# Attention on one core: row maximum of q.k alone in four row groups, the weighted sum in two pieces per head

## The reference

```python
qkv = (x @ w_qkv).reshape(B, L, 3, H, Dh)            # B=4, L=1024, H=16, Dh=8
attn = jnp.einsum('bhid,bhjd->bhij', q, k) * Dh ** (-0.5)
attn = attn + phi_bias(L)[None, None]                # log(exp(-|p_i - p_j|) + 1e-8)
attn = jax.nn.softmax(attn, axis=-1)
out = jnp.einsum('bhij,bhjd->bhid', attn, v)
out = jnp.transpose(out, (0, 2, 1, 3)).reshape(B, L, D)
return out @ w_proj + b_proj
```

## Time and profile before

| | us |
|---|---|
| median of 3 runs | 1227.99 |
| lowest and highest | 1227.91, 1228.85 |
| span of the profiled execution | 1235.2 |
| attend stage, first to last issue of a store | 224.7 to 272.1 |
| attention, first score matmul to last weighted sum | 273.4 to 1016.9 |
| steps 1 to 61 of it | 302.3 to 992.1 |

### The profile page before, as it was taken

How to read it: one execution, slowest core, us unless ns; L and a number is a source line. 1 busy time by engine, 2 the same in 40 slices (tenths; PEclk the granted TensorE clock), 3 DMA queues, 4 the chain that set the end, 5 groups by cost and what they waited for, 6 DMA issues and landing times. The chain is left out here.

```text
span 1235.2 us, 26880 instructions
## 1 busy us (share of the span) xinstructions
PE 1084.3 (88%) x6562; PEld 529.4 (43%) x6563; DVE 933.5 (76%) x1753; ACT 708.5 (57%) x1574; POOL 419.9 (34%) x628
## 2 busy tenths in 40 slices
PE   5549993759999999999999999999999986729997
PEld 4449993422222222222222222222222216629997
DVE  6447774869888888888888888888888817837885
ACT  1024441444777777777777777777777761104443
POOL 2524343443223332323232333323232322642433
PEclk9999997787999999999999999999999996659999
DMA  9221113240111111111111111111111146432221
GB/s 329 97 55 44 41 43 88 96 148 20 30 34 37 32 31 34 36 31 32 35 35 31 31 36 33 31 33 36 32 31 35 28 103 202 164 109 69 67 67 30
DMA packets 54063, 77.03 MB, mean 62 GB/s; under 512 B 15679, under 2 KB 35269, under 8 KB 53368
## 3 DMA queue, kind: packets, MB, share of 16 engines
q1 hardware_dynamic: 48264, 65.25, 18.0%
q0 software_dynamic: 5056, 10.53, 2.3%
q10 hardware_dynamic: 704, 0.79, 0.3%
HBM read 54.61 MB, written 25.41 MB: 65 GB/s over the span
## 5 line engine op out<-in xcount | busy, mean ns | idle before, releaser
L946 DVE TENSOR_REDUCE nmax<-psS 128x1 f32<-128x1024 f32 x512 | 602.9, 1220 | 109.2 <-PE psS L899 109.1
L960 ACT ACTIVATE prob<-psE 128x512 f32<-128x512 f32 x1024 | 537.1, 606 | 179.2 <-PE psE L891 178.9
L899 PE MATMUL psS<-kop,qop 120*128 120x512 bf16 x1024 | 393.8, 388 | 11.6 <-DVE mpart L930 8.6
L891 PE MATMUL psE<-qop,kop 123*128 123x512 bf16 x1024 | 389.1, 382 | 3.4 <-ACT prob L960 2.6
L1004 POOL TENSOR_TENSOR prob<-prob,const 128x512 f32<-128x512 f32 x128 | 162.4, 1269 | 472.5 <-ACT prob L960 472.5
L915 PE MATMUL psV<-prob,vst 128*9 128x512 f32 x2048 | 267.1, 595 | 1.0 <-issue 0.8
L891 PEld LDWEIGHTS psE<-qop,kop 123*128 123x128 bf16 x1024 | 99.3, 98 | 314.1 <-ACT prob L960 219.0
L899 PEld LDWEIGHTS psS<-kop,qop 120*128 120x128 bf16 x1024 | 99.5, 98 | 117.7 <-DVE nmax L946 17.7
L752 ACT ACTIVATE siga<-psGa,w1sa 128x128 f32<-128x128 f32 x156 | 44.5, 368 | 62.9 <-PE psGa L660 62.9
L752 ACT ACTIVATE sigb<-psGb,w1sb 128x128 f32<-128x128 f32 x156 | 44.5, 368 | 60.7 <-PE psGb L660 60.7
L915 PEld LDWEIGHTS psV<-prob,vst 128*9 128x9 f32 x2048 | 30.8, 88 | 109.9 <-issue 109.9
(11 more groups left out here) (163 smaller groups left out, 1023.2 us busy)
## 6 DMA issues: line engine op xcount, KB each, us to landing
qop<-qk_parts SPq DMA_DIRECT2D x192, 48.0 KB
kop<-qk_parts SPq DMA_DIRECT2D x192, 48.0 KB
qk_parts<-part_attend SPq DMA_DIRECT2D x16, 384.0 KB, 2.8
xsb<-sorted_b SPq DMA_DIRECT2D x39, 128.5 KB
weighted_sums<-osum SPq DMA_DIRECT2D x256, 18.0 KB
w1a<-in_w SPq DMA_DIRECT2D x1, 4128.0 KB
w1b<-in_w SPq DMA_DIRECT2D x1, 4128.0 KB
qop<-mrow SPq DMA_DIRECT2D x256, 1.5 KB
```

The lines of the kernel that those rows point to most:

```text
L891: nc.tensor.matmul(psE[BANK[n]][:], kop[b][0:TROWS, kt * P:(kt + 1) * P], qop[b][0:TROWS, cols], start=True, stop=True).then_inc(s_t, 1)
L899: last = nc.tensor.matmul(psS[kt % 2][:, half, :], qop[b][0:SROWS, kt * P:(kt + 1) * P], kop[b][0:SROWS, cols], start=True, stop=True)
L946: nc.vector.tensor_reduce(nmax[r % 2][:, qt:qt + 1], psS[qt % 2][:], AX.XY, ALU.max, negate=True).then_inc(s_max, 1)
L960: nc.scalar.activation(prob[r % 2][:, lo:lo + HALF], psE[BANK[n]][:], ACT.Exp).then_inc(s_exp, 1)
```

## The change

The scores for the maximum no longer contain the bias, and of q and k only four of the nine products of parts: low.low, high.high, high.middle and middle.high. These are 32 rows, and they stand four times in new operands `qS` and `kS` of 128 partitions: the two halves of an even tile and those of an odd tile use the rows from 0, 32, 64 and 96 on. The row maximum is thus that of q.k alone, and it goes into the exponent in two bf16 parts instead of three (122 rows, two removed GpSimd operations). q and k are stored with their parts in sequences ("lhhml" and "hmlhmh") in five and six transfers per group, and every operand of a head comes with one transfer: four per head instead of six, of 256, 256, 144 and 144 KB. The sums are stored whole, with the unused partitions, in one transfer, and read back in eight per batch instead of four. TensorE's order is now by pairs of tiles: exponents of the even tile, scores of both tiles, exponents of the odd tile, and after every second pair two pieces of the weighted sum. In the diff, counts of semaphores and the shape of `pickhead` and `kbias`, which follow from this, are left out.

```diff
@@ -32,8 +32,10 @@
 COMBO = 9 * DH
 BIAS0, BIASN = COMBO, 6 * KT
 MAX0 = BIAS0 + BIASN
-SROWS = MAX0
-TROWS = MAX0 + 3
+TROWS = MAX0 + 2
+QSEQ, KSEQ = "lhhml", "hmlhmh"
+STORES = len(QSEQ) + len(KSEQ)
+SROWS = 4 * DH
 PBLK = L + P
 
 XBUF = 4
...
@@ -261,13 +263,14 @@
                     sp.dma_start(g.kop[n][BIAS0:TROWS, :], d.kbias).then_inc(g.s_init, 16)
                 for n in range(groups):
                     b, c = half(n)
-                    for z in range(2):
+                    for z, (to, seq) in enumerate(((d.q, QSEQ), (d.k, KSEQ))):
                         sp.wait_ge(s_part, 2 * n + z + 1)
-                        sp.dma_start(d.qk[z, :, b * P:(b + 1) * P, c].rearrange("a p t -> p a t"),
-                                     part[:, n % 2, z, :, :]).then_inc(s_out[n % 2], 16)
+                        for at, a in enumerate(seq):
+                            sp.dma_start(to[b * HEADS:(b + 1) * HEADS, at, :, c],
+                                         part[:, n % 2, z, "hml".index(a), :]).then_inc(s_out[n % 2], 16)
                     if n == 1:
                         for s in range(2):
-                            sp.wait_ge(s_out[s], 32)
+                            sp.wait_ge(s_out[s], 16 * STORES)
                     if n in (2, 4, 6):
                         load_head(sp, d, g, n // 2 - 1, n // 2 - 1)
             if not attend:
...
@@ -763,21 +766,27 @@
 
 def load_sums(sp, d, g, b):
 
-    sums = d.sums.rearrange("(b h) a e t -> b a h e t", h=HEADS)
-    for a in range(2):
-        sp.dma_start(g.den[:, b % 2, a, :], sums[b, a, :, DH, :].rearrange("h (j q) -> h j q", q=P))\
-            .then_inc(g.s_den_in[b], 16)
-        sp.dma_start(g.num[:, b % 2, a, :], sums[b, a, :, 0:DH, :]).then_inc(g.s_num_in[b], 16)
+    sums = d.sums.rearrange("(b h) (j e) t -> b j h e t", h=HEADS, j=4)
+    for j in range(4):
+        a, half = j // 2, j % 2
+        sp.dma_start(g.den[half * 64:half * 64 + 64, b % 2, a, :],
+                     sums[b, j, :, DH, :].rearrange("h (j q) -> h j q", q=P)).then_inc(g.s_den_in[b], 16)
+        sp.dma_start(g.num[:, b % 2, a, half * HALF:(half + 1) * HALF], sums[b, j, :, 0:DH, :])\
+            .then_inc(g.s_num_in[b], 16)
 
 
 def load_head(sp, d, g, head, b):
 
-    rows = bass.ds(head * DH, DH)
-    for a in range(3):
-        at = slice(a * 3 * DH, (a + 1) * 3 * DH)
-        sp.dma_start(g.qop[b][at, :], d.qk[0, a, rows, :].unsqueeze(0).to_broadcast([3, DH, L])
-                     ).then_inc(g.s_op[b], 16)
-        sp.dma_start(g.kop[b][at, :], d.qk[1, :, rows, :]).then_inc(g.s_op[b], 16)
+
+    def rows(src, at, parts, repeat, step):
+        size = len(QSEQ if src is d.q else KSEQ) * DH * L
+        return bass.AP(tensor=src.tensor, offset=head * size + at * DH * L,
+                       ap=[[step * DH * L, repeat], [L, parts * DH], [1, L]])
+
+    sp.dma_start(g.qS[b][:], rows(d.q, 0, 4, 4, 0)).then_inc(g.s_op[b], 16)
+    sp.dma_start(g.kS[b][:], rows(d.k, 2, 4, 4, 0)).then_inc(g.s_op[b], 16)
+    sp.dma_start(g.qop[b][0:COMBO, :], rows(d.q, 2, 3, 3, 0)).then_inc(g.s_op[b], 16)
+    sp.dma_start(g.kop[b][0:COMBO, :], rows(d.k, 0, 3, 3, 1)).then_inc(g.s_op[b], 16)
 
 
 def phase_attention(nc, d, g):
...
@@ -848,10 +857,8 @@
 
                 if live(at, -2):
                     sp.wait_ge(s_ev, i - 1)
-                    for j in range(4):
-                        sp.dma_start(d.sums[bass.ds(i - 2, 1), j // 2, :,
-                                            (j % 2) * HALF:(j % 2 + 1) * HALF].squeeze(),
-                                     osum[r % 2][32 * j:32 * j + VW, :]).then_inc(s_os[r % 2], 16)
+                    sp.dma_start(d.sums[bass.ds(i - 2, 1), :, :].squeeze(),
+                                 osum[r % 2][:]).then_inc(s_os[r % 2], 16)
 
                 if live(at, 1):
                     b = (r + 1) % NBUF
...
@@ -860,16 +867,16 @@
 
                         sp.dma_start(qop[b][MAX0:TROWS, :].rearrange("a (t q) -> a t q", q=P)
                                      [:, :, 32 * u:32 * u + 32],
-                                     mrow[(r + 1) % 2][32 * u:32 * u + 3 * KT, :]).then_inc(s_mr[b], 16)
+                                     mrow[(r + 1) % 2][32 * u:32 * u + 2 * KT, :]).then_inc(s_mr[b], 16)
 
...
@@ -878,46 +885,64 @@
             pe.wait_ge(s_one, 5)
 
             def step(i, r, at, q):
-                for kt in range(KT):
+                def weigh(kt):
+
+                    b = r % NBUF
                     for half in range(2):
-                        cols = slice(half * HALF, (half + 1) * HALF)
-                        if live(at, 0):
-                            b, n = r % NBUF, 2 * kt + half
-                            if n == 0:
-                                pe.wait_ge(s_mr[b], 64 * filled(q, r, 0))
-
-                            if later(at, 0, 1) or n >= BANK_AGE[n]:
-                                pe.wait_ge(s_exp, 16 * i + n + 1 - BANK_AGE[n])
-                            nc.tensor.matmul(psE[BANK[n]][:], kop[b][0:TROWS, kt * P:(kt + 1) * P],
-                                             qop[b][0:TROWS, cols], start=True, stop=True).then_inc(s_t, 1)
-                        if live(at, 2):
-                            b = (r + 2) % NBUF
-                            if kt == 0 and half == 0:
-                                pe.wait_ge(s_op[b], 96 * filled(q, r, 2))
-                            if half == 0 and (later(at, 2, 1) or kt >= 2):
-                                pe.wait_ge(s_max, 8 * (i + 2) + kt - 1)
-                            last = nc.tensor.matmul(psS[kt % 2][:, half, :],
-                                                    qop[b][0:SROWS, kt * P:(kt + 1) * P],
-                                                    kop[b][0:SROWS, cols], start=True, stop=True)
-                            if half == 1:
-                                last.then_inc(s_s, 1)
-                    if kt % 2 == 1 and live(at, -1):
-
-                        if kt == 1:
-                            pe.wait_ge(s_vst, i)
-                            if later(at, -1, 1):
-                                pe.wait_ge(s_ev, i - 1)
-                        if kt in (1, 5):
-                            pe.wait_ge(s_diag, 2 * i - 1 + kt // 4)
-                            pe.wait_ge(s_exp, 16 * i - 8 + 8 * (kt // 4))
-                        for j in range(4):
-                            k, half = kt - 1 + j // 2, j % 2
-                            last = nc.tensor.matmul(
-                                psV[32 * j:32 * j + VW, :], vst[(r + 1) % 2][:, k, :],
-                                prob[(r + 1) % 2][:, k * PBLK + half * HALF:k * PBLK + (half + 1) * HALF],
-                                start=(kt == 1), stop=(kt == 7))
-                        if kt == 7:
-                            last.then_inc(s_pv, 1)
+                        n = 2 * kt + half
+                        if n == 0:
+                            pe.wait_ge(s_mr[b], 64 * filled(q, r, 0))
+
+                        if later(at, 0, 1) or n >= BANK_AGE[n]:
+                            pe.wait_ge(s_exp, 16 * i + n + 1 - BANK_AGE[n])
+                        nc.tensor.matmul(psE[BANK[n]][:], kop[b][0:TROWS, kt * P:(kt + 1) * P],
+                                         qop[b][0:TROWS, half * HALF:(half + 1) * HALF],
+                                         start=True, stop=True).then_inc(s_t, 1)
+
+                def score(qt):
+
+                    b = (r + 2) % NBUF
+                    if qt == 0:
+                        pe.wait_ge(s_op[b], 64 * filled(q, r, 2))
+                    if later(at, 2, 1) or qt >= 2:
+                        pe.wait_ge(s_max, 8 * (i + 2) + qt - 1)
+                    for half in range(2):
+                        lo = 32 * (qt % 2 * 2 + half)
+                        last = nc.tensor.matmul(psS[qt % 2][:, half, :],
+                                                qS[b][lo:lo + SROWS, qt * P:(qt + 1) * P],
+                                                kS[b][lo:lo + SROWS, half * HALF:(half + 1) * HALF],
+                                                start=True, stop=True)
+                    last.then_inc(s_s, 1)
+
+                def gather(p):
+
+                    if p == 0:
+                        pe.wait_ge(s_vst, i)
+                        if later(at, -1, 1):
+                            pe.wait_ge(s_ev, i - 1)
+                    if p in (0, 2):
+                        pe.wait_ge(s_diag, 2 * i - 1 + p // 2)
+                        pe.wait_ge(s_exp, 16 * i - 8 + 8 * (p // 2))
+                    for j in range(4):
+                        k, half = 2 * p + j // 2, j % 2
+                        last = nc.tensor.matmul(
+                            psV[32 * j:32 * j + VW, :], vst[(r + 1) % 2][:, k, :],
+                            prob[(r + 1) % 2][:, k * PBLK + half * HALF:k * PBLK + (half + 1) * HALF],
+                            start=(p == 0), stop=(p == 3))
+                    if p == 3:
```

(54 more changed lines are left out.)

## The result

The changed kernel takes 1302.98 us (median of 4 runs, 1302.17 to 1304.00) and the kernel before 1228.42 in the same runs: 1.0616 times the time, 95% interval 1.0599 to 1.0632. The forecast was 1307 us.

What follows compares the result with a forecast made beforehand. TensorE was taken to set the pace before; after the change, the larger of TensorE-VectorE chain and loads. Loop +60, attend stage +20, ends +0.6 and -1.3 gave +79: 1307 us against the 1228.0 median, range 1255 to 1368.

Steps and rivals of the forecast that it cites:

- The chain: Attention loop: odd tile's score to VectorE's next start 3.63 us, a round of four tiles 6.05, a head 12.10 against 11.31.
- Lower and upper bound: Chain per head: 11.74 us if changing rows costs nothing, 12.98 if the matmuls of one pair run one after another.
- VectorE's idle time: Sign in the attention loop: VectorE idle near 2.8 us per head (170 us), with the score matmul as releaser.
- Two of the signs: Loop: 3.6 us gap between two VectorE starts each round; a head's first exponent matmul released by the maxima row's transfer.
- The loads: Attention loop: maxima row queues behind loads and store, next head's exponent matmul waits; 12.3 us per head, +60 over 61 steps.
- The bound with rows of 80 ns: Loop of the loads: lower bound of 11.2 us per head, with 80 ns rows and no start costs.
- The attend stage: Eleven stores per group instead of two, 0.64 us per issue on SyncE: +21 us worked out, +20 taken.
- The ends: Steps 62 and 63: doubled piece adds 0.3 us each; last store issued once, -1.3; loads of the sums 0.
- VectorE setting the pace (1): Rival in the attention loop: scores always ready before VectorE asks, 9.5 us per head, 1138 us in all; chance 0.13.
- Loads (2): Rival in the attention loop: loads decide fully, 13.1 us per head, 1358 us in all; chance 0.17.
- Row groups not side by side (3): Rival for the score matmuls: row groups don't run side by side, 12.98 us per head, 1350 us; chance 0.10.
- The clock (4): Rival for TensorE in the loop: a tenth of heads at 1.2 GHz, 18 us each, +41, 1348 us; chance 0.09.

Runs made afterwards that it cites:

- e3: The kernel before with the weighted sum in two pieces per head instead of four, all else unchanged; 1284.1 us, 1.045 of the kernel before.
- e4: The changed kernel with all score matmuls in rows 0 to 31, so no two run side by side; 1402.8 us, 1.142 of the kernel before.
- e5: The changed kernel with four weighted-sum pieces per head and each copy of qS and kS loaded by its own transfer; 1253.5 us, 1.015 of the kernel before.
- e2: The changed kernel with each copy of qS and kS loaded by its own transfer over sixteen engines; 1311.2 us, 1.069 of the kernel before.
- e7: The changed kernel with three of eleven attend-stage stores per group issued by ScalarE instead of SyncE; 1307.7 us, 1.057 of the kernel before.
- e6: e5 with the maxima row and store issued before the loads, and copies loaded for head i+4; 1222.6 us, 0.987 of the kernel before.
- e1: The changed kernel with the weighted sum again in four pieces per head, one behind each pair of tiles; 1282.9 us, 1.043 of the kernel before.

## Why the prediction came out right, step by step

**The chain (right).** Predicted 3.63 us from the odd tile's score to VectorE's next start and a round of 6.05; measured 3.67 (653.29 to 656.96) and 6.07. Its parts, predicted in brackets: score pair and way back 0.33 (0.32), one exponent matmul to the next and to the weighted sum 0.53 (0.52), two pieces 1.84 (1.84), the next two exponent matmuls to the scores 0.54 (0.52), to VectorE 0.43 (0.43). The column-group borders of the earlier trace rows priced the row-group borders within 0.02. e3 shows that the double piece is the cause, and e4 that the row groups do what they say. Lower and upper bound were both further off than the value taken.

**VectorE's idle time (right).** 2.8 us per head foretold, 173.6 us / 61 = 2.8 found. Two of the signs named with it aren't there. Between two VectorE starts the longest gap of a round is 2.67 us (654.29 to 656.96), not 3.6; 3.63 is the way from the odd tile's score to VectorE's start. And only five times in the 61 steps does the profile show a first exponent matmul or its weight load held by the maxima row.

**The loads (wrong in size, and so in rank).** The step that failed is the loop of the loads, 12.3, which I let decide over 12.10. In the profile the DMA share is 0.26 while the copied loads run and 0.20 in the loads of three parts, so four and three engines as predicted. Up to the last packet of the maxima row the sum was nearly right: 10.8 after the step's first exponent matmul by the prediction, 10.5 in the step from 655.99 on (666.5), 10.1 to 11.4 over the loop with a median of 10.7. In a full queue a row costs 0.084 us (four engines at 100 GB/s give 0.082) and no start costs show. The term that was too large is the last, 1.50 from the last packet to TensorE: in the three long steps of the changed kernel, in which the matmul really waited for the row, it started 1.03 to 1.09 after the last packet, and in e5, where it waits in most steps, 0.9. With 1.05 the loop is 11.7 to 11.8 and stands 0.4 behind the chain, and e2 shows that relieving it changes nothing.

The 0.088 also doesn't come from where the prediction says. 335 GB/s over sixteen engines make 0.098 us for a row of 2 KB, by which the loop would have been 13.5; that 0.088 lies near the measured 0.084 is luck. The bound with rows of 80 ns comes to 11.4, not 11.2.

The forecast had +60 us for the loop; +53.3 was found, 12.10 alone would have given +48. The remaining 0.08 per head over 12.10 is 0.05 from two rounds of 6.07 to 6.08 instead of 6.05, 0.02 from every fourth step, which takes 12.22 (in e2 too), and 0.01 from three steps of 12.3 to 12.5, in which the wait for the maxima row does show (3.1 us in all, over five waits).

**The attend stage (right).** +21 worked out, +20 taken, +21.5 found; SyncE's stores take 0.64 us from issue to issue (3.24 for five, 3.85 for six):

```profile
215.79 3.24 SPq L269 DMA_DIRECT2D q_parts<-part_attend  x5
219.07 3.85 SPq L269 DMA_DIRECT2D k_parts<-part_attend  x6
...
239.01 0.69 SPq L786 DMA_DIRECT2D qS<-q_parts  x1
...
280.87 3.83 SPq L269 DMA_DIRECT2D k_parts<-part_attend  x6
```

But the reason isn't SyncE alone: e7 takes 15 us of its issues away and gains 6. The prediction's +21 was added up from SyncE's issues; the 64 us that it gave the shared DMA engines stood beside the sum, and e7 speaks for them.

**The ends.** -0.7 foretold, +1.5 found up to the last weighted sum and -2.7 after it; the latter is no more than runs differ there.

**The rivals.** VectorE setting the pace (1): out; it is idle for 2.8 us per head here, for want of scores, and for 1.0 even with four pieces and the loads out of the way (e6). Loads (2): out by e2 here, but in force in e1, one edit away. Row groups not side by side (3): out by e4. The clock (4): 1.00 in the whole loop of the changed kernel, out; it came in e1 and e4. Its price was too high: a tenth of the heads at 18 instead of 12.3 is +35 on 1307, 1342; the +41 counts from the 11.31 of the kernel before.

Against the profiled executions the sum of +79 is 6 us high: the loads' term was 7 too large, the stage's 1.5 too small, the ends' 2.2 too small up to the last weighted sum, and the 2.7 behind it weren't in it. Against the medians (+74.6) it is 4 to 5 high. The misses partly cancel, so that the total is this close is in part luck.

## What to carry to other kernels

A piece of work may be merged with its neighbour only if the engine that lives on what is queued behind it has buffers for that long: here two buffers hold 2.36 us of VectorE's work, and the doubled piece keeps TensorE away for longer, which costs 0.9 us per head however cheap the scores become. To price such an edit, write down the loop through the smallest buffer, edge by edge from the rows, beside the sums of each engine's work; the sums alone said the contrary. A change that takes the longest loop away must be costed with the second one, here the small transfer queued behind large loads on few DMA engines.

## What the runs showed of the hardware that I had not expected

- With all scores in 32 rows of one row group TensorE's clock fell to 1.2 GHz again and again, though the engine was busy for 2.37 of the 2.50 us from 652.0 on in e4 and for 3.08 of the 3.30 us up to the fall at 655.3; with the same matmuls side by side in four row groups and TensorE idle for 13% of the loop it stayed at 2.4 GHz. Four row groups don't hold it there by themselves: in e1, with the same score matmuls, it fell too, and there TensorE had stood idle before (1.82 us for the maxima row up to 652.97, the fall at 654.4). So idle time goes before the falls of e1 and not before those of e4, and a busy engine in the profile doesn't by itself say that the clock stays up. Which property of the work decides in e4 wasn't tried.
- A weight load of 128 columns in another row group costs nothing that shows here: four loads and four matmuls of 512 columns are through in 0.40 us (656.53), and one such matmul lasts 0.385.
- Four copies in one issue aren't spread like 128 partitions in one: the copied loads ran at a DMA share of 0.26, four engines of sixteen, at 100 GB/s, where stores from 128 partitions reached 1.01. The Trainium skill (DMA: Bandwidth & Descriptors, How many engines) states the rule by which they take four; the traces agree.
